# Units of one node over 128-edge parts in the dense message layer: 62 supersteps in place of 74, built by 49-column products

## The reference, cut to what matters

```
loops = arange(n_nodes)
ei = concatenate([edge_index, stack([loops, loops])], axis=1)
col, row = ei[0], ei[1]
in_deg  = segment_sum(1, col);  out_deg = segment_sum(1, row)
ew = out_deg[row]**-0.5 * in_deg[col]**-0.5
y_forward  = segment_sum((x @ W_f.T)[row] * ew[:, None], col)   # sum over edges, to the source node
y_backward = segment_sum((x @ W_b.T)[col] * ew[:, None], row)   # sum over edges, to the target node
y = concatenate([y_forward, y_backward], axis=-1) + bias_param
```

## Time and profile before

| | us |
|---|---|
| median of 3 runs | 6537.67 |
| lowest, highest | 6533.43, 6541.74 |
| profiled execution | 6540.98 |
| its span, first to last instruction | 6539.1 |
| TensorE busy | 4807.3 (74%) |
| VectorE busy | 3625.1 (55%) |
| ScalarE busy | 1736.2 (27%) |
| GpSimd busy | 2140.0 (33%) |

### The profile page before, as it was taken

How to read it: one execution, slowest core, us unless ns; L and a number is a source line. 1 busy time by engine, 2 the same in 40 slices (tenths; PEclk the granted TensorE clock), 3 DMA queues, 4 the chain that set the end, 5 groups by cost and what they waited for, 6 DMA issues and landing times. The chain is left out here.

```text
span 6539.1 us, 84391 instructions
## 1 busy us (share of the span) xinstructions
PE 4807.3 (74%) x25224; PEld 3437.6 (53%) x25225; DVE 3625.1 (55%) x7583; ACT 1736.2 (27%) x3028; POOL 2140.0 (33%) x2163
## 2 busy tenths in 40 slices
PE   1544676676666676767469963799999999977993
PEld 0432444444444444444358852566666666656873
DVE  6943454545454454545861137777777777763114
ACT  0022222222222222222112234333333333322121
POOL 1005566556566565656004423000000000021220
PEclk9986666666667766666679986899999999976997
DMA  3365455555555554545226661333333333332333
GB/s 88 63 217 124 128 138 130 137 131 138 130 135 134 129 136 128 138 129 133 65 66 207 208 205 54 80 78 82 74 75 74 80 80 74 75 88 95 106 120 102
DMA packets 1040972, 747.82 MB, mean 114 GB/s; under 512 B 815268, under 2 KB 926748, under 8 KB 1038717
## 3 DMA queue, kind: packets, MB, share of 16 engines
q1 hardware_dynamic: 937917, 457.79, 26.2%
q0 software_dynamic: 102848, 287.97, 16.6%
HBM read 480.57 MB, written 91.62 MB: 88 GB/s over the span
## 5 line engine op out<-in xcount | busy, mean ns | idle before, releaser
L1041 POOL DMA_INDIRECT gat_rows<-h_rows,gat_sources x1664 | 1577.1, 948 | 1061.9 <-issue 499.8
L1279 PE MATMUL gat_sum_ps<-gat_rows,gat_onehot 128*128 128x265 f32 x3328 | 1395.1, 576 | 469.5 <-issue 281.8
L1279 PEld LDWEIGHTS gat_sum_ps<-gat_rows,gat_onehot 128*128 128x128 f32 x3328 | 904.3, 286 | 744.4 <-issue 536.6
L1679 ACT CAST gnn_z<-build_ps 128x392 bf16<-128x392 f32 x1184 | 567.4, 486 | 1106.3 <-PE build_ps L1694 1095.7
L1694 PE MATMUL build_ps<-onehot_code,onehot_low 128*128 128x196 bf16 x4736 | 594.7, 250 | 158.0 <-DVE onehot_code L1621 138.7
L1704 PE MATMUL back_ps<-zb_pieces,gnn_z 128*128 128x384 bf16 x3626 | 672.8, 325 | 0.0
L1726 PE MATMUL front_ps<-x_res_wide,front_rows 128*128 128x448 bf16 x3108 | 669.3, 352 | 0.0
L1694 PEld LDWEIGHTS build_ps<-onehot_code,onehot_low 128*128 128x128 bf16 x4736 | 432.8, 98 | 334.8 <-issue 138.0
L1598 POOL DMA_INDIRECT front_rows<-zf_piece_rows,vrow_nodes x74 | 88.9, 1201 | 1555.3 <-PE front_ps L1726 1543.5
L1621 DVE TENSOR_TENSOR onehot_code<-dense_codes,code_pattern 128x1568 bf16<-128x1568 bf16 x592 | 573.6, 969 | 0.0
L1633 DVE TENSOR_TENSOR gnn_z<-gnn_z,front_ps 128x448 f32<-128x448 f32 x518 | 321.9, 621 | 398.7 <-PE front_ps L1726 398.5
(11 more groups left out here) (350 smaller groups left out, 5337.2 us busy)
## 6 DMA issues: line engine op xcount, KB each, us to landing
moe_w<-in_L_ffn_W SPq DMA_DIRECT2D x112, 512.0 KB
gat_targets<-gat_step_targets SPq DMA_DIRECT2D x104, 512.0 KB
moe_w<-in_L_ffn_w SPq DMA_DIRECT2D x32, 1024.0 KB
gat_rows<-h_rows,gat_sources POOLq DMA_INDIRECT x1664
moe_taken<-moe_rows_out SPq DMA_DIRECT2D x21, 896.0 KB, 7.1
moe_rows_out<-gat_slot_zeros SPq DMA_DIRECT2D x36, 512.0 KB
gat_flags<-gat_tile_flags SPq DMA_DIRECT2D x104, 128.0 KB
normal_rows<-moe_xn_all SPq DMA_DIRECT2D x14, 896.0 KB, 4.0
```

The source lines that it names most:

```text
L1041: pool.indirect_dma_start(out=g[:, b, t, :], out_offset=None, in_=T.h[:, :], in_offset=bass.IndirectOffsetOnAxis(ap=idx[:, b, t:t + 1], ax ...
L1279: last = pe.matmul(po[:, s % BANKS, 0:W], o[:, b, s * SUB + t, :], g[:, b, s * SUB + t, :], start=t == 0, stop=t == SUB - 1)
L1679: nc.scalar.copy(AT[:, k % 2, :, 2 * QUAD * c:2 * QUAD * (c + 1)].rearrange("p h (u d) -> p h u d", u=2), pb[:, c % 2, 0:2 * CW].rearrange ...
```

## The change

- A unit is now one *part* of 128 edges with one node. Edge rows are written to DRAM per part. The code of an edge in a unit is (node minus the unit's node) times 49 plus h: 49 values. A superstep holds 128 units, one vrow each. Parts plus nodes give 62 supersteps.
- A step c builds 8 units with one matmul each, 49 columns, no accumulation; the copy by ScalarE still takes 392 columns. The table of the code pattern goes; both one-hots use the iota table (2048 and 784 elements for two steps, in place of 1024 and 1568).
- The unit table is no longer searched. For each part the number of its units is worked out, a running sum and one matmul give the place of its first unit, and GpSimd scatters a step (1, and 1 where no node is shared with the part before) to this place of a zeroed table in DRAM, 128 parts at a time, 13 times. SyncE loads the table; TensorE sums it up (three products), VectorE scans 62 columns, and part and node of each unit follow. The attention layer's table is worked out as before.
- The count's steps are dealt out anew: two behind each of the 7 step groups, the other 98 over the 62 unit groups. There are 62 gathers into a ring of 16 buffers, in place of 19 gathers into buffers of their own.

```diff
-        self.GROUPS = self.ROWS // QUAD
+        self.PARTS = -(-self.E // P)
+        self.PG = -(-self.PARTS // P)
         self.BATCH = -(-(self.BLOCKS + self.NT) // STEPS)
         self.SG = -(-(self.BATCH * STEPS + STEPS) // P)
-        self.SUPER = 2 * -(-(self.BLOCKS + -(-self.N // QUAD)) // (2 * UNITS))
-        self.BATCHES = -(-self.SUPER * UNITS // P)
-        self.CODES = QUAD * self.NT
+        self.SUPER = 2 * -(-(self.PARTS + self.N) // (2 * P))
+        assert self.ROWS > self.N and self.PG * P <= self.BG * P * (BLK // P)
         assert self.NT == GROUP * GROUP
         self.G1 += self.G1 % 2
         self.G2 += self.G2 % 2
...
+            def halves(a):
+                return T.gnn.rearrange("(g p t) (a e) -> p g t a e", p=P, t=SUB, a=2)[:, :, :, a, :]
+
+            def split(t):
+                return t[:, :, :].rearrange("p g (t e) -> p g t e", t=SUB)
             stores = [(4, rows(T.gat, 0), sf[:, :, :]), (5, rows(T.gat, 1), df[:, :, :]),
                       (7, T.hi[:, :], hi[:, :]), (7, T.lo[:, :], lo[:, :]),
                       (10, rows(T.gat, 2), fs[:, :, :]), (10, rows(T.gat, 3), fe[:, :, :]),
-                      (10, rows(T.gnn, 0), val[:, :, :]), (10, rows(T.gnn, 1), low[:, :, :])]
+                      *[(10, halves(a)[:, :, t, :], split(data)[:, :, t, :]) for a, data in enumerate((val, low)) for t in range(SUB)]]
             for n, out, data in stores:
...
+            sp.wait_ge(pd, 1)
+            for out, data in part_loads:
+                sp.dma_start(out, data, allow_slow_non_contiguous=True).then_inc(ul, 16)
+            sp.wait_ge(zr, 1)
+            sp.dma_start(T.steps.rearrange("(p f) c -> p (f c)", p=P), zero[:, :]).then_inc(zd, 16)
             count.load(sp)
...
+            sp.wait_ge(us, 16 * PG)
+            sp.dma_start(us_r[:, :, :], T.steps[0:NQ * P, :].rearrange("(s p) c -> p s c", p=P),
+                         allow_slow_non_contiguous=True).then_inc(ur, 16)
...
+            pool.wait_ge(zd, 16)
+            pool.wait_ge(ui, 1)
+            for j in range(PG):
+                pool.indirect_dma_start(
+                    out=T.steps[:, :], out_offset=bass.IndirectOffsetOnAxis(ap=pl[:, j:j + 1], axis=0),
+                    in_=pv[:, j, :], in_offset=None).then_inc(us, 16)
...
-            for j in range(NJ):
+            for s in range(NQ):
+                if s >= RING:
+                    pool.wait_ge(tp, s - RING + 1)
                 pool.indirect_dma_start(
-                    out=vr[:, j, :, :].rearrange("p a e -> p (a e)"), out_offset=None, in_=T.gnn[:, :],
-                    in_offset=bass.IndirectOffsetOnAxis(ap=bk_i[:, j:j + 1], axis=0)).then_inc(rg[j], 16)
+                    out=vr[:, s % RING, :, :].rearrange("p a e -> p (a e)"), out_offset=None, in_=T.gnn[:, :],
+                    in_offset=bass.IndirectOffsetOnAxis(ap=bk_i[:, s:s + 1], axis=0)).then_inc(rg[s % RING], 16)
...
+            dve.wait_ge(ul, 16 * len(part_loads))
+            dve.wait_ge(pd, 1)
+            dve.wait_ge(zr, 1)
+            c.link(dve.tensor_copy(pe_f[:, :, :], pe_i[:, :, :]))
+            c.link(dve.tensor_tensor(pv[:, :, 1], pe_f[:, 0, :], pe_f[:, 2, :], ALU.is_equal))
+            c.link(dve.tensor_tensor(pn[:, :], pe_f[:, 1, :], pe_f[:, 2, :], ALU.subtract))
+            c.link(dve.tensor_tensor(pn[:, :], pn[:, :], pv[:, :, 1], ALU.add))
+            c.link(dve.tensor_tensor_scan(pc[:, :], zero[:, 0:PG], pn[:, :], 0.0, ALU.add, ALU.add))
+            dve.nop(nofuse=True).then_inc(ut, 1)
+
             dve.wait_ge(ld, 64)
...
+            dve.wait_ge(uo, 1)
+            c.link(dve.tensor_tensor(pn[:, :], pc[:, :], pn[:, :], ALU.subtract))
+            c.link(dve.tensor_scalar(pl[:, :], pn[:, :], pg[:, A_OFF:A_OFF + 1], None, ALU.add))
+            dve.nop(nofuse=True).then_inc(ui, 1)
+
+            dve.wait_ge(bp, 1)
+            for n in range(4):
+                a, (lo, hi) = n // 2, cuts[n % 2]
+                c.link(dve.tensor_copy(wide[:, a, lo:hi], pw[:, n, 0:hi - lo]))
...
-            spread(1)
-            place(1, NJ, bk, sk)
-            c.link(dve.tensor_copy(bk_i[:, :], bk[:, :]))
-            c.link(dve.tensor_tensor(g[:, :], kn[:, :], sk[:, :], ALU.subtract))
-            c.link(dve.tensor_scalar(g[:, :], g[:, :], float(S.GROUPS - 1), None, ALU.min))
-            c.link(dve.tensor_scalar(gc[:, :], g[:, :], float(S.CODES), None, ALU.mult))
-            dve.nop(nofuse=True).then_inc(bi, 1)
...
-                dve.wait_ge(rg[j], 16)
-                dve.tensor_scalar(vr[:, j, 0, :], vr[:, j, 0, :], gc[:, j:j + 1], None, ALU.subtract).then_inc(cr, 1)
-                for t in counted(SG + j):
+
+            dve.wait_ge(uc, 1)
+            for a in range(2):
+                c.link(dve.tensor_tensor_scan(uf[:, a, 1:NQ + 1], zero[:, 0:NQ],
+                                              pg[:, A_COL:A_COL + 2 * NQ].rearrange("p (s c) -> p c s", c=2)[:, a, :], 0.0,
+                                              ALU.add, ALU.add))
+            c.link(dve.tensor_tensor(ug[:, :, :], pg[:, A_SUM:A_SUM + 2 * NQ].rearrange("p (s c) -> p c s", c=2),
+                                     uf[:, :, 0:NQ], ALU.add))
+            c.link(dve.tensor_scalar(bk_i[:, :], ug[:, 0, :], 1.0, None, ALU.subtract))
+            c.link(dve.tensor_tensor(ug[:, 1, :], kn[:, :], ug[:, 1, :], ALU.subtract))
+            c.link(dve.tensor_scalar(ug[:, 1, :], ug[:, 1, :], float(S.ROWS - 1), None, ALU.min))
+            c.link(dve.tensor_scalar(gc[:, :], ug[:, 1, :], float(W), None, ALU.mult))
+            dve.nop(nofuse=True).then_inc(bi, 1)
+            for s in range(NQ):
+                dve.wait_ge(rg[s % RING], 16 * (s // RING + 1))
+                dve.tensor_scalar(vr[:, s % RING, 0, :], vr[:, s % RING, 0, :], gc[:, s:s + 1], None,
+                                  ALU.subtract).then_inc(cr, 1)
+                for t in counted(SG + s):
                     count.onehots(dve, t)
             c.mark(count.keep(dve, pw[:, 0, 0:S.NT]))
...
+            pe.wait_ge(ut, 1)
+            pe.matmul(pg[:, A_OFF:A_OFF + 1], C.upper[:, :], pc[:, PG - 1:PG], start=True, stop=True).then_inc(uo, 1)
...
+            pe.wait_ge(ur, 16)
+            steps = us_r[:, :, :].rearrange("p s c -> p (s c)")
+            pe.wait_ge(ui, 1)
+            pe.matmul(pg[:, A_SUM:A_SUM + 2 * NQ], C.upper[:, :], steps, start=True, stop=False)
+            pe.matmul(pg[:, A_SUM:A_SUM + 2 * NQ], C.ident[:, :], steps, start=False, stop=True)
+            pe.matmul(pg[:, A_COL:A_COL + 2 * NQ], C.ones[:, :], steps, start=True, stop=True).then_inc(uc, 1)
...
-                at = slice(2 * HITS * c, 2 * HITS * (c + DUO))
-                for out, table, w, a in ((ol, io_b, P, 1), (oj, pat, CW, 0)):
-                    shape = [P, QUADS, w, HITS]
+                at = slice(CHUNK * c, CHUNK * (c + DUO))
+                for out, w, a in ((ol, P, 1), (oj, NT, 0)):
+                    shape = [P, PAIRS, w, HITS]
                     last = dve.tensor_tensor(out[:, n, :, :, :],
                                              ct[:, k % SLOTS, a, at].rearrange("p (u t) -> p u t", t=HITS).unsqueeze(2)
                                              .to_broadcast(shape),
-                                             table[:, :, :].unsqueeze(1).to_broadcast(shape), ALU.is_equal)
+                                             io_b[:, 0:w, :].unsqueeze(1).to_broadcast(shape), ALU.is_equal)
...
-                        nc.scalar.copy(AT[:, k % 2, :, 2 * QUAD * c:2 * QUAD * (c + 1)].rearrange("p h (u d) -> p h u d", u=2),
-                                       pb[:, c % 2, 0:2 * CW].rearrange("p (u h d) -> p h u d", u=2, d=QUAD)).then_inc(ae, 1)
+                        nc.scalar.copy(AT[:, k % 2, :, CHUNK * c:CHUNK * (c + 1)],
+                                       pb[:, c % 2, 0:CHUNK * NT].rearrange("p (u h) -> p h u", u=CHUNK)).then_inc(ae, 1)
...
-                for u in range(2):
-                    for t in range(2):
-                        last = pe.matmul(pb[:, c % 2, u * CW:(u + 1) * CW], ol[:, n, c % DUO * 2 + u, :, t],
-                                         oj[:, n, c % DUO * 2 + u, :, t], start=t == 0, stop=t == 1)
+                for u in range(CHUNK):
+                    i, t = (c % DUO * CHUNK + u) // HITS, u % HITS
+                    last = pe.matmul(pb[:, c % 2, u * NT:(u + 1) * NT], ol[:, n, i, :, t], oj[:, n, i, :, t],
+                                     start=True, stop=True)
```

296 lines of the change are left out of this document (146 added, 150 removed).

## The result

| | before | after |
|---|---|---|
| median of 4 runs, us | 6535.55 (6529.77 to 6541.74) | 6280.07 (6278.73 to 6287.78) |
| profiled execution, its span | 6540.98, 6539.1 | 6280.63, 6278.8 |
| end of the tables stage | 355.9 | 345.7 |
| VectorE's first dense one-hot | 4118.95 | 4106.45 |
| end of the dense layer | 5806.2 | 5546.8 |

The ratio is 0.9615, with a 95% interval of 0.960 to 0.963: 255 us faster, where 363 were forecast. Of the 260 us between the profiled executions the dense layer has 247 (1687.3 to 1440.3), the tables stage 10, the rest of the kernel 3.

What follows compares the result with a forecast made beforehand. TensorE's time per superstep was taken to bound the dense stage. Dense layer −341 and tables stage −25 gave −366 on 6540.98, so 6175; the median of runs lies 3.3 lower, 6172 us. Range 6125 to 6265.

Steps and rivals of the forecast that it cites:

- Supersteps and builds: Dense layer: 62 supersteps for 74; eight 49-column pairs at 28 ns make a build step 0.244 us, 0.111 less.
- rival 1: Dense builds: short pairs stay issue bound at 37 to 42 ns, only fewer supersteps count; 6249 us, 20%.
- rival 3: Dense builds: weight loads partly bare, 48 ns a pair gives 6284 us, 60 ns gives 6361 us; 6%.
- rival 4: Dense builds: whole weight load bare at 98 ns a pair, so the change is slower; 6641 us, 3%.
- The 42 ns: Dense builds: upper bound for a 49-column pair, read from the count in the tables stage at the slow level.
- Over 59 supersteps: Dense stage: every full superstep at 21.47 us gives 1267 us against 1610, so 343 us less.
- The turn chain: Superstep turn in the dense layer: VectorE's longer one-hots add 0.13 us; the merge wait grows from 0.31 to about 0.6.
- ScalarE's copy: Dense builds: copy reads single words 49 apart; 0.48 us now, even 0.8 us would fit, so no effect.
- Tables stage: Stage before the dense layer: fewer searches against new bare waits, 25 us less, bounds −40 to +20.
- The first gather lands 5.3 us after issue: Tables stage: the landing, hidden by searches before, becomes bare, so the count starts at 115.5 against 149.66.
- The chain behind the early count: Tables stage, after 14 early count steps: step-sum products, seven small operations and a first gather, about 9 us bare.
- Rival 2: Tables stage gives nothing or loses 20 us to bare DMA waits; 6197 to 6217 us, 5%.

Runs made afterwards that it cites:

- e1: The changed kernel with TensorE's dense-layer loop written out for all 62 supersteps, other engines still looping; 5588.97 us, ratio 0.9373.
- e9: The changed kernel with TensorE's loop written out, plus two PSUM banks for the back sums and the merge two builds later; 6119.51 us, ratio 0.936.
- e13: The changed kernel with the store of the step windows (896 pieces of 4 bytes) moved behind the third gather's use; 264.8 us faster than the kernel before.
- e5: The changed kernel itself, run again beside the kernel before as the measure for neighbouring runs; ratio 0.9577.
- e7: The changed kernel with eight supersteps in TensorE's loop body in place of four; ratio 0.9393, 362 us faster than the kernel before.
- e10: The changed kernel with five supersteps ahead of TensorE's loop in place of four, body length kept; 6211.24 us.
- e8: The changed kernel with TensorE's loop cut in the middle of a superstep, between eighth and ninth build; ratio 0.9462, 321 us faster than the kernel before.
- e2: The kernel before with eight supersteps in TensorE's loop body in place of four; ratio 1.0012, 6.9 us slower than the kernel before.
- e4: The changed kernel with the load of the unit table (8-byte pieces) issued after the third gather's use; 255.9 us faster than the kernel before.
- e14: The changed kernel with unit table load after the second gather and window store after the fourth; 254.7 us faster than the kernel before.

## Why the prediction was wrong, by its steps

The forecast, 6172 us, was 108 us too low, and the time lies outside the range of 6125 to 6265.

- **Supersteps and builds: right.** Eight builds take 0.38 us and 15 take 0.58 (rows above), so a pair costs (0.58 − 0.19)/14 = 0.028 us, as taken. Rivals 1, 3 and 4 fell. The 42 ns were the price at the lower clock, as the prediction read them: at a granted clock of 0.50, from 4825.07 on, the changed kernel's own pairs start 41 to 44 ns apart. But 28 was picked between the bounds and not worked out, so its exactness is partly luck. The same ratio as the f32 transposes of the earlier trace rows, 421 to 272 ns, would have given 42 × 272/421 = 27. The 37 ns in rival 1 no run shows: the 16 pairs of the earlier trace rows ran at a granted clock of 0.50 and so say nothing of the fast level, and their starts are 43 to 47 and 77 to 88 ns apart in turn, so the register instruction of every second pair adds some 35 to a pair of 45. The block is 2.70 us for 2.75. The plain superstep has 21.25 on average against 21.47; over 59 that is 13 us on the good side. VectorE is busy 80% of the stage for 83.
- **"Over 59 supersteps": the step that failed.** The sum took every superstep as plain. Thirteen are not: they are 28.2 to 30.9 us, together 384.5, where e1 has 21.3 each, 276.9. That is +108 us, the whole miss. The forecast priced 128 pairs instead of 64 by TensorE's time and never by their number of instructions, which grows a loop body from 628 to 884 matmuls (5.4 to 7.4 blocks). e1 shows the price directly: 118 us. Nothing in my rivals held it; rival 3's 6284 is near the measured time by chance, since its price of 48 ns a pair isn't there. Small slips in the sums change nothing: by its own terms rival 3 at 60 ns is 6354 and not 6361, rival 4 is 6638 and not 6641, and 4 × 196 columns at the slope are 0.329 us and not 0.335.
- **The turn chain: right in direction.** The merge waits 0.7 to 0.9 us in place of 0.31, VectorE named, forecast 0.6. e9 shows that it could be had: 47 us.
- **ScalarE's copy: right.** 487 ns for 0.48; reading words 49 apart costs nothing.
- **Tables stage: −10 in place of −25.** The first block instruction came at 74.7 (forecast 77) and the chain to the gather took 31.0 us (32.4), so issue was 4 us early. "The first gather lands 5.3 us after issue" failed: 13.3, by the window store (e13), and the count starts 4.5 us late at 120.0. The chain behind the early count took 7.6 us for 9. The other part is idle time inside the count: I expected half of the 9 us to go, and VectorE has 15.8 us of it (two waits of 8.3 and 6.6, one put down to issue; their cause is open, and e5, the same kernel, has waits of 2.7 and 2.6 us there instead). And the 62 adds take 0.20 each from start to start, not 0.15, 3 us more.
- **Rival 2** (bare waits in the tables stage) had the right mechanism for those 15 us, at a fraction of the 25 to 45 that it took.

The miss adds up: +108 (turns) − 13 (plain supersteps) + 15 (tables) − 3 (the rest of the kernel) = 107, against 108 measured.

What stays open is why the second block after the jump is asked for so late: 4.6 to 6.9 us after the first in the changed kernel, e7 and e10, 3.4 to 4.5 in e8, 3.1 to 3.7 in e2, some 8 beside a plain copy. That the stall it makes depends on how many of the loop's instructions lie in the first block is shown by e10's counts.

## What to carry to other kernels

Count instructions as well as microseconds: an edit that halves the columns and doubles the matmuls also lengthens each loop body, and past some six blocks of 256 instructions turns begin to fetch their code again (some of them at 6.5, every one at 7.4). The view to read is the instruction queue's packets in a stretch of the loop: near zero is safe, one block for every 256 instructions of the body is not. Then write the loop out, or make the body much longer so that there are fewer jumps. And look at what is issued just ahead of a transfer that an engine waits for barely: one store in single words, of 3.5 KB, held up the first gather behind it by 8 to 9 us.

## What the runs showed of the hardware that was not expected

- Code that streams in without jumps is free for TensorE even at 457 instructions in 21.2 us (e1); a taken jump to code that is not at hand stops it for 2.1 to 2.8 us (e7, e8, e10; 1.3 to 1.7 in e2), and up to 7.2 us more at the next block. Each of these stalls ends 2.2 to 3.6 us after the start of an instruction packet.
- A stall costs more than itself. After two stalls with 0.6 us of work between them the granted clock was at 0.50 in each of the 13 turns, for 6.8 to 10.2 us that begin in the second stall, and six front pairs take 2.45 us in place of 1.29. After a single stall of 2.1 to 2.7 us it fell in some turns only, for 3.4 us (8 of 13 in e8, 1 of 5 in e7), and after e2's of 1.3 to 1.7 in none.
- Weight load and matmul pairs of 49 columns go at 28 ns at the clock of 1.00 and 41 to 44 at a granted 0.50, a ratio of 1.5 for half the clock.
- Two small-piece transfers issued 0.4 us apart act quite differently on a gather beside them: the store of 896 pieces of 4 bytes delays it by 8 to 9 us (e4 against e14), and taking away the load of 7936 pieces of 8 bytes gains it 2 at most (e4 against e5).
